# The first steps of a cross-attention kernel: lead-in in another order, first pair's weights loaded from ScalarE's queue

## The reference

```python
# L0: twice (weights 1, then 2); H=16 heads of K=128
h  = layer_norm(x)                       # over D=256
qh = (h @ wq + bq); kh = (ctx @ wk + bk); vh = (ctx @ wv + bv)      # 16 heads each
kh, vh = one more row each (bias_k, bias_v)
w  = softmax(qh . kh / sqrt(128))
x  = x + (w . vh) @ wo + bo
# then  x = x + gelu(layer_norm(x) @ w_fc1 + b) @ w_fc2 + b
# L1, L2, L3: smaller attentions over the same x, not touched
```

## Time and profile before

| | us |
|---|---|
| median of 3 runs | 2310.05 |
| lowest, highest | 2309.37, 2313.97 |
| profiled execution, its own time | 2313.7 |
| its span, first to last instruction | 2312.0 |
| PE busy | 2175.6 (94%) |
| DVE busy | 1572.7 (68%) |
| ACT busy | 1576.6 (68%) |
| POOL busy | 730.9 (32%) |

### The profile page before, as it was taken

One profiled execution on the slowest core, in us unless ns is written; L12 is line 12 of the kernel. 1 busy time (PEld: TensorE's weight loads), 2 busy tenths in 40 slices (PEclk: granted clock), 3 DMA queues, 4 the chain that ended last, 5 costly groups with the idle time before them and its releaser, 6 DMA issues. The chain is left out here.

```text
span 2312.0 us, 51787 instructions
## 1 busy us (share of the span) xinstructions
PE 2175.6 (94%) x17289; PEld 1768.3 (76%) x17289; DVE 1572.7 (68%) x4008; ACT 1576.6 (68%) x4490; POOL 730.9 (32%) x1029
## 2 busy tenths in 40 slices
PE   5999999999999999997989999789999989899998
PEld 4899999998999999996976665456666679666664
DVE  6555555557555555556758999687777666799986
ACT  3666666665666666665637787577788766487875
POOL 1111111113311111102124565377777720334310
PEclk9999999999999999998979999799999999799999
DMA  5001111100010110001000000100000000000001
GB/s 133 24 24 24 24 24 46 37 11 15 24 24 24 24 25 24 1 2 51 22 8 10 9 11 6 38 8 1 6 15 17 14 8 5 7 10 11 8 4 37
DMA packets 72938, 47.08 MB, mean 20 GB/s; under 512 B 29232, under 2 KB 71600, under 8 KB 72752
## 3 DMA queue, kind: packets, MB, share of 16 engines
q1 hardware_dynamic: 72752, 44.62, 7.5%
HBM read 41.45 MB, written 2.10 MB: 19 GB/s over the span
## 5 line engine op out<-in xcount | busy, mean ns | idle before, releaser
L2051 DVE TENSOR_REDUCE maxima<-bank 128x2 f32<-128x512 f32 x512 | 332.9, 682 | 34.9 <-PE bank L1049 32.7
L1619 ACT ACTIVATE probs_t<-bank 128x512 f32<-128x512 f32 x512 | 282.4, 601 | 65.2 <-PE bank L1040 63.5
L1911 DVE SCALAR_TENSOR_TENSOR wide_heads_low<-bank,wide_columns,wide_heads_high 128x128 fp32r<-128x128 f32 x512 | 155.8, 346 | 216.0 <-ACT wide_heads_high L1484 216.0
L1472 ACT ACTIVATE wide_probs<-bank,wide_neg_max 128x129 f32<-128x129 f32 x512 | 183.8, 364 | 117.2 <-DVE wide_neg_max L1891 112.3
L2406 POOL TENSOR_TENSOR wide_columns<-wide_pair_columns,zero 128x8 f32<-128x8 f32 x16 | 3.3, 203 | 711.7 <-DVE x L1924 669.3
L1467 ACT ACTIVATE wide_probs_t<-bank 128x256 f32<-128x256 f32 x256 | 98.0, 383 | 165.1 <-PE bank L911 163.3
L1478 ACT ACTIVATE wide_probs<-wide_probs,wide_inverse 128x128 f32<-128x128 f32 x464 | 161.6, 396 | 53.9 <-DVE wide_inverse L1895 53.9
L1895 DVE RECIPROCAL wide_inverse<-wide_sums 128x2 f32<-128x2 f32 x256 | 42.5, 166 | 226.4 <-ACT wide_probs L1472 226.4
L1049 PE MATMUL bank<-k_packed,q_packed 32*128 32x256 f32 x1024 | 176.1, 343 | 4.1 <-ACT q_packed L1604 2.2
L1040 PE MATMUL bank<-q_packed,k_packed 32*128 32x256 f32 x1024 | 169.9, 334 | 8.2 <-ACT probs_t L1619 7.4
L1656 ACT ACTIVATE probs<-scores_masked,neg_max 128x128 f32<-128x128 f32 x512 | 163.2, 393 | 10.7 <-DVE neg_max L2230 9.9
(11 more groups left out here) (316 smaller groups left out, 6803.8 us busy)
## 6 DMA issues: line engine op xcount, KB each, us to landing
cn<-in_ctx SPq DMA_DIRECT2D x48, 128.0 KB, 2.0
wide_pair_weights<-in_L_xattn_wq SPq DMA_DIRECT2D x16, 256.0 KB, 2.8
wide_pair_weights<-in_L_xattn_wk SPq DMA_DIRECT2D x16, 256.0 KB, 3.2
wide_pair_weights<-in_L_xattn_wv SPq DMA_DIRECT2D x16, 256.0 KB, 3.7
wide_pair_weights<-in_L_xattn_wo SPq DMA_DIRECT2D x16, 256.0 KB, 3.4
q_packed<-max_rows SPq DMA_DIRECT2D x256, 4.0 KB
wide_ctx_rows<-in_ctx SPq DMA_DIRECT2D x4, 512.0 KB, 6.4
x<-in_x SPq DMA_DIRECT2D x4, 512.0 KB, 7.3
```

The costliest lines, as they stand in the source:

```text
L1472: last = act.activation(probs0[:, b, h, :], wide_scores[b % 2][:, h * KEYS0:(h + 1) * KEYS0], ACT.Exp, bias=neg_max0[:, b, h:h + 1], accum ...
L1619: act.activation(probs_t[j % 8][:, :], shifted_bank[j % 2][:, :], ACT.Exp, bias=0.0).then_inc(s.exp_ready, 1)
L1911: last = dve.scalar_tensor_tensor(heads_low[:, h, a, :], wide_heads[a % 2][:, h * P:(h + 1) * P], columns[slot][:, 3, h:h + 1], heads_high ...
L2051: dve.tensor_reduce(maxima[pack // 2][:, b, pack % 2, :], head_scores[packed_scores(1 - u, j)][:, :].rearrange("p (a k) -> p a k", a=UNITS ...
```

## The change

The first pair's ten loads are issued by ACT, ahead of everything else on its queue, with the weights of K first. SP loads x before the context of group 0. Only groups 0 and 1 are prepared before the first scores; the projections of step 0 start as soon as group 0's context and K's weights are there (K, then Q, then V), with group 1's transposes and the context of groups 2 and 3 put between them. The normed rows of groups 2 and 3 go through the path that was there for the second layer: statistics in `window(-1)` and `window(0)`, transposes and copies by halves in `window(0)` and `window(1)`, roots and low parts on POOL, scaling of probabilities by DVE in `window(0)` and `window(1)`. The roots of groups 0 and 1 are POOL's too. POOL makes the first pair's low weights one kind at a time. `first_bias` runs once per step in steps 0 to 3. ACT and DVE get their first eight steps unrolled.

```diff
+CTX_BANKS = (0, 2, 2, 4)
-        looped(1, last // 2 - span + 1)
+        fixed(1, span + 1)
+        looped(span + 1, last // 2 - span + 1)
+def renewed(g, back):
+    if not isinstance(g, int):
+        return None
+    first, second = g - back + GROUPS - 1, g - back - (SECOND - GROUPS + 1)
+    if SLOTS <= first < GROUPS:
+        return first
+    return GROUPS + second if 0 <= second < GROUPS else None
 # PE
+            def first_projections():
+                pe.wait_ge(ctx_low_ready, DC)
+                pe.wait_ge(preparation_steps, 4)
+                for piece in (2, 3):
+                    project(0, 0, 0, piece)
+                turn_normed(1)
+                pe.wait_ge(normed_low_ready, DC)
+                pe.wait_ge(preparation_steps, 7)
+                for piece in (0, 1):
+                    pe.wait_ge(k_copied, piece + 1)
+                    project(0, 0, 0, piece)
+                turn_context(2)
+                pe.wait_ge(weights_split, 2)
+                for piece in (4, 5):
+                    pe.wait_ge(q_copied, piece - 3)
+                    project(0, 0, 0, piece)
+                turn_context(3)
 # ACT
         def norm_and_split():
+            load_first_pair()
             split_context(0)
-            for g in range(GROUPS - 1):
-                split_context(g + 1)
-                split_normed(g)
-                if g == 0:
-                    first_weights()
+            split_context(1)
+            first_weights((1, 0))
+            split_normed(0)
+            first_weights((2, 3))
 # DVE
+            norm_steps(0, 0)
+            norm_steps(0, 1)
             split_context(0)
-            for g in range(GROUPS - 1):
-                norm_group(g)
-                split_context(g + 1)
-                if g:
-                    split_normed(g - 1)
+            norm_steps(0, 2)
+            norm_steps(0, 3)
+            split_context(1)
+            norm_steps(1, 0)
+            norm_steps(1, 1)
+            split_normed(0)
+            norm_steps(1, 2)
+            norm_steps(1, 3)
+            norm_steps(2, 0)
+            norm_steps(2, 1)
+                if not core and not carry:
+                    copy_queries(0, 0, 0)
+                    copy_queries(0, 0, 1)
+                    split_normed(1)
+                    norm_steps(2, 2)
+                    norm_steps(2, 3)
+                    copy_values(0, 0, 0)
+                    split_context(2)
+                    copy_values(0, 0, 1)
+                    return
-                    if core and not carry:
-                        first_bias(b)
                     if ended is not None:
-                        norm_second(ended, b)
+                        norm_steps(ended, b)
+                    if core and b == 2 and isinstance(g, int) and g < GROUPS:
+                        first_bias(g)
 # POOL
+            pool.wait_ge(weights_split, 1)
+            root(0)
+            pool.wait_ge(pair_loaded, 16 * PAIR_LOADS)
+            copy(columns[0][:, :, :], pair_columns[:, :, :]).then_inc(preparation_steps, 1)
+            weights_low_of(1, 1).then_inc(preparation_steps, 2)
+            root(1)
+            weights_low_of(0, 2).then_inc(preparation_steps, 2)
+            weights_low_of(2, 3).then_inc(preparation_steps, 2)
+            weights_low_of(3, 4).then_inc(preparation_steps, 2)
...
+            root(2)
+            low(2, 0)
+            root(3)
+            low(2, 1)
+            low(3, 0)
+            low(3, 1)
-        split_pair(0, 0, first=True)
-        split_pair(1, 1)
+        first_pair()
+        split_pair(1, 1, GROUPS)
 # SP
+        load_x(0)
         load_context(0)
-        load_x(0)
...
-        load_pair(0, 0, 0)
```

More of the change, by code:

```diff
@@ L861, in project @@
                 tok = slice(n * TOK, (n + 1) * TOK)
-                if piece == 0 and n == 0:
-                    pe.wait_ge(weights_split, pair + 2)
-                if kind == 0:
-                    if not isinstance(gg, int) or gg > 0:
+                if gg:
+                    if piece == 0 and n == 0:
+                        pe.wait_ge(weights_split, pair + 2)
+                    if kind == 0:
                         pe.wait_ge(v_copied, 2 * gg - 1 + half)
-                else:
-                    pe.wait_ge((q_copied, k_copied)[kind - 1], 2 * gg + half + 1)
+                    else:
+                        pe.wait_ge((q_copied, k_copied)[kind - 1], 2 * gg + half + 1)
                 if kind < 2:
@@ L892, in window @@
                     if ready is not None and b == 0:
-                        pe.wait_ge(normed_low_ready, DC * (GROUPS + ready + 1))
+                        pe.wait_ge(normed_low_ready, DC * (ready + 1))
+                    if not carry and b == 0:
+                        pe.wait_ge(ctx_low_ready, DC * SLOTS)
+                        pe.wait_ge(normed_low_ready, DC * SLOTS)
+                    if not carry and b == 1:
+                        pe.wait_ge(ctx_low_ready, DC * GROUPS)
                     if core:
@@ L1421, in split_half @@
             for c in range(DC):
-                ins = act.activation(normed[:, c, part], wide_heads[b % 2][:, c * D:(c + 1) * D], ACT.Identity, bias=norm_offset[:, 1, c:c + 1],
-                                     scale=norm_scale[:, 1, c:c + 1])
+                ins = act.activation(normed[:, c, part], wide_heads[b % 2][:, c * D:(c + 1) * D], ACT.Identity, bias=norm_offset[:, norm, c:c + 1],
+                                     scale=norm_scale[:, norm, c:c + 1])
             ins.then_inc(normed_ready, 1)
@@ L2454, in split_pair @@
             pool.wait_ge(x_added, 8 * (p - 1) + ADD_CREDIT)
-            if isinstance(p, int) and p == 1:
-                pool.wait_ge(normed_low_ready, DC * GROUPS)
             chain.mark(copy(columns[slot][:, :, :], pair_columns[:, :, :]))
-            if first:
-                chain.steps += 4
-                chain.join()
             for kind in range(4):
-                if not first:
-                    chain.link(copy(wh[:, kind, :], pair_weights[:, kind, :]))
+                chain.link(copy(wh[:, kind, :], pair_weights[:, kind, :]))
                 chain.mark(pool.tensor_tensor(wl[:, kind, :], pair_weights[:, kind, :], wh[:, kind, :].bitcast(F32),
```

196 lines of the change are left out of this document (103 added, 93 removed).

## The result

| us | before | after |
|---|---|---|
| median, lowest to highest (4 runs each, same chip) | 2311.89, 2309.37 to 2313.97 | 2295.98, 2290.73 to 2298.61 |
| profiled execution, its span | 2313.7, 2312.0 | 2298.61, 2296.9 |
| the same pair on another chip (11 and 6 runs) | 2308.24, 2306.93 to 2314.34 | 2295.74, 2293.83 to 2299.65 |

The changed kernel is faster by 0.7 and 0.6%: ratio 0.9934 [0.9918, 0.9950], on the other chip 0.9942 [0.9929, 0.9956]. That is 16 and 12.5 us, where 22 were forecast; 2296 is the forecast range's upper end.

What follows compares the result with a forecast made beforehand. PE bounds the steady part, so only an earlier step 3 counts: first scores at 31, plus 16.6, 17.65, 16.2 and 1 us margin, give 82.4 for 104.63. A gain of 22 us from the median 2310.05 gives 2288, range 2283 to 2296.

Steps and rivals of the forecast that it cites:

- The landing: Lead-in: the last of the first pair's ten weight loads lands at 15 us, between 13.4 and 17, for 16.56 before.
- The first rival: Lead-in loads: weights land no sooner (17), x and context later; gain 18 to 20 us, time 2291, chance 0.23.
- Group 1's rows in time at 21.1: Lead-in: group 1's normed rows are ready at 21.1 us, before PE ends K's projection and its transposes need them.
- No wait of PE over 1 us, the clock stays up: From K's projection to the first scores, PE waits at most 1 us at a time and keeps its upper clock level.
- The rest of the chain: Lead-in: from K's projection ending at 21.5, through transposes, Q and V, to first scores at 31 us.
- Steps 0 to 2: First three steps after the first scores: 16.6, 17.65 and 16.2 us, against 15.68 for a steady step.
- the margin of 1 us: Added to the sum up to step 3's start for waits not found: 81.45 becomes 82.4 us.
- The seam: Existing steps with preparation, taken as model for steps 0 and 1: three at 18.58 us, the last 17.15, against 15.68.
- The bias, at most 0.5 a step: Steps 1 to 3: DVE's bias of 1.2 us, now one per step, costs at most 0.5 us in each.
- the mark: Start of step 3, where the sum closes: 82.4 us for 104.63 before, 22.2 us earlier.
- The second pair's split: POOL's split of the second pair's weights ends at 74.6 us, PE wants it in step 3 at 81.4; cover 6.8.
- the second rival: Steps 0 and 1 and lead-in: DVE's queues collide or PE's clock stays low; gain 11 us, time 2299, chance 0.10.

Runs made afterwards that it cites:

- the second trace: The changed kernel run again with nothing changed, on the same chip: ratio 0.9942 [0.9929, 0.9956] to the kernel before, first scores at 37.36 us.

## Why the prediction missed by a third

- **The landing** (15, bounds 13.4 to 17): wrong, at 19.46 outside its bounds, and the first step to fail. I took the last load's 6.1 us from issue to landing from before and counted the bytes of the ten loads. But the change also lets PE's first transposes release context 2 and x of group 2 into the same engines (with them held back, the landing came at 15.99, inside the bounds), and puts all of the weights beside contexts 0 and 1. K begins at 21.59 for 17.2: 4.4 us. From the landing to K, 2.1 us for 2.2, the chain was right. The first rival had the rule right and its size too small.
- **Group 1's rows in time at 21.1**: wrong. They came at 28.5. Part is the landing, that of x of group 1 too (statistics from 18.36, for x at 16); 2.7 us are PE's wait on top, because I priced DVE's operations at 1.28 and 1.38, their length alone. The trace of before had the same operations beside the same POOL work:

```profile
18.90 2.33 DVE L1791 TENSOR_SCALAR wide_rows<-x,mean_var,rstd 128x256 f32<-128x256 f32 x4
21.15 1.28 DVE L1743 TENSOR_TENSOR wide_ctx_low<-bank,wide_ctx_high 128x512 fp32r<-128x512 f32 x2
22.35 1.79 DVE L1834 TENSOR_TENSOR wide_normed_low<-wide_normed,wide_normed_high 128x512 fp32r<-128x512 f32 x1
...
32.37 1.29 DVE L1834 TENSOR_TENSOR wide_normed_low<-wide_normed,wide_normed_high 128x512 fp32r<-128x512 f32 x2
```

  with POOL on its low parts from 19.68 to 25.27: rows 2.33 for 1.38 and one low part 1.79 for 0.64 (half of the 1.29 that two take with POOL idle), while the operation that reads one input from a bank kept its length. The rows were in that trace, and I didn't read them.
- **No wait of PE over 1 us, the clock stays up**: wrong. In this trace PE waited 2.65 and the clock cost 2.8 us. In the second one PE waited 1.64 and the clock was at 0.50 through K's projection, but up behind it, so it cost the first scores little: the rows of group 1 came last anyway. It should have been a range of 0 to 3 us and not a fixed term.
- The rest of the chain, from group 1's transposes to the scores: 9.5 forecast (21.5 to 31), 9.02 in the second trace. Right. Together 31 + 4.4 + 2.7 + 2.8 − 0.5 = 40.4.
- **Steps 0 to 2**: 16.6, 17.65 and 16.2 forecast, 16.45, 17.64 and 15.69 measured. Right, and the margin of 1 us wasn't needed. The seam was a good model.
- **The bias, at most 0.5 a step**: 0.56 in step 1, then 1.0 each, showing one step later than I put it, so 2 us behind the mark at which I closed the sum. DVE's maximum stood right behind it in the queue; 1.2 us of work behind a short gap costs what the gap doesn't hold.
- **The second pair's split** (end 74.6, needed 81.4): it ended at 84.84, PE was there at 90.2 and didn't wait. Both moved by about the 9.4 us of the first scores; the cover was 5.4 us for 6.8, enough.
- **The mark**: 22.2 − 9.4 + 1.6 = 14.4 at step 3, as measured (17.5 in the second trace). The bias takes 2.0 more. The medians' 16 and 12.5 us are near the 12.4 to 15.4 us of the marks at step 5. The profiled pair's 15.1 holds 2.7 us of luck: by so much the rest of the program happened to be shorter (2173.3 for 2176.0).

In short: the terms that failed are the landing, put at 15 and measured at 19.46, DVE's operations, put at 2.66 and measured at 6.16 beside POOL, and the clock, put at nothing and measured at 2.8. The median of 2295.98 still lies in the range of 2283 to 2296, at its very edge, and that bears out none of them. The direction, the bound and the way in which a lead-in is priced were right; the second rival had named the right places (waits and low clock, gain 11), at a chance that was too low.

## What to carry to other kernels

When loads move to an earlier place, draw up everything that shares the DMA engines until they land, those included that the change itself releases, and wait for each piece where it is needed, not for all of them. Before you price a VectorE operation by its row, look whether GpSimd was busy beside that row, and whether it will be in the new place. Extra work on an engine belongs into a wait ahead of the operation that others wait for.

## What the runs showed of the hardware

VectorE's rows stood still while GpSimd's subtractions ran (3.76 us for 1.37 beside 2.54 us of GpSimd), and GpSimd lost nothing in that place; its three subtractions beside VectorE's low parts and rows took 4.72 us for 3.8. VectorE's low part that reads one input from a bank kept its length, 0.64. TensorE's clock level in the first 35 us wasn't fixed by the code: two executions of the same kernel differed by 2.8 us through it. 18 transposes in the wait ahead of it gave K's projection 0.40 us a product from its second one on; without them its first six took 0.63 to 0.76. And ten loads issued from 0.8 us on landed later, at 18.9 to 19.5 in five traces, than the same ten issued behind x of group 1 on the other queue, at 18.1 in one; with a megabyte held back they landed at 16.0.
